# Second mixer's outputs: 32-partition chunk matrices turned by VectorE, 32x32 state tiles, two corrected chunks a step

## The reference, cut to what matters

```python
def step(s, inp):
    q_, w_, k_, v_, a_, b_ = inp
    sa = jnp.einsum('bhij,bhj->bhi', s, a_)
    s = s * w_[:, :, None, :] + sa[..., None] * b_[:, :, None, :] + v_[..., None] * k_[:, :, None, :]
    return (s, jnp.einsum('bhij,bhj->bhi', s, q_))
_, y = jax.lax.scan(step, s0, (qt, wt, kt, vt, at, bt))
...
y = ((yg - mu) / jnp.sqrt(var + EPS)).reshape(Bx, Tx, C) * ln_w + ln_b
y = y + (rk * v.reshape(Bx, Tx, H, HS)).reshape(Bx, Tx, C)
return y * g @ Wo.T
```

## Time and profile before

| what | value |
|---|---|
| median of 3 runs | 5464.05 us |
| the three runs | 5441.55, 5478.0, 5464.05 us |
| the profiled execution, first to last instruction | 5452.6 us |
| mean granted TensorE clock of it (1.0 is 2.4 GHz) | 0.926 |
| the changed stage in it | 4295.36 to 4500.67 us, 205.3 us |

### The profile page before, as it was taken

One profiled execution on the slowest core, in us unless ns is written; L12 is line 12 of the kernel. 1 busy time (PEld: TensorE's weight loads), 2 busy tenths in 40 slices (PEclk: granted clock), 3 DMA queues, 4 the chain that ended last, 5 costly groups with the idle time before them and its releaser, 6 DMA issues. The chain is left out here.

```text
span 5452.6 us, 104905 instructions
## 1 busy us (share of the span) xinstructions
PE 4831.1 (89%) x36890; PEld 3535.1 (65%) x36890; DVE 3836.5 (70%) x9111; ACT 2736.9 (50%) x6711; POOL 2285.8 (42%) x1860
## 2 busy tenths in 40 slices
PE   5999999999999999999889989984488778998998
PEld 3787777877777787777766556641156665654665
DVE  4766667777677766767578668746699657866874
ACT  2444445444544544545478658724400116875882
POOL 2434334344334434434267347514322116743751
PEclk7999999999999999999999999986699758998998
DMA  2000000000000000000100000000000000000000
GB/s 86 5 9 7 7 9 7 7 9 7 7 9 10 5 9 8 6 9 9 34 1 0 25 5 0 0 7 0 8 1 1 1 1 30 0 24 5 0 0 16
DMA packets 170085, 52.60 MB, mean 10 GB/s; under 512 B 142304, under 2 KB 166112, under 8 KB 168928
## 3 DMA queue, kind: packets, MB, share of 16 engines
q1 hardware_dynamic: 168160, 44.30, 3.7%
q10 hardware_dynamic: 1536, 3.21, 0.2%
HBM read 36.99 MB, written 10.49 MB: 9 GB/s over the span
## 5 line engine op out<-in xcount | busy, mean ns | idle before, releaser
L799 DVE SCALAR_TENSOR_TENSOR gd_qkT<-gd_ps,gd_w_qk,gd_qkT 128x256 f32<-128x256 f32 x768 | 367.2, 482 | 193.3 <-ACT gd_qkT L632 172.7
L984 POOL TENSOR_TENSOR gd_gV<-gd_g,cst 128x512 f32<-128x512 f32 x128 | 130.3, 1040 | 860.1 <-PE gd_ps L510 860.1
L417 PE MATMUL gd_ps<-gd_taps,gd_xwins 128*128 128x512 f32 x1024 | 465.3, 597 | 0.0
L676 ACT ACTIVATE gd_X<-gd_ps 128x512 f32<-128x512 f32 x384 | 201.1, 620 | 452.9 <-PE gd_ps L496 452.6
L1540 ACT ACTIVATE L_ffn_s<-L_ffn_s,L_ffn_nb,L_ffn_r 128x128 f32<-128x128 f32 x1024 | 419.4, 482 | 3.1
L1360 POOL TENSOR_TENSOR L_ffn_t<-L_ffn_t 128x512 f32<-128x512 f32 x128 | 190.2, 1486 | 391.8 <-DVE L_ffn_t L1581 391.8
L417 PEld LDWEIGHTS gd_ps<-gd_taps,gd_xwins 128*128 128x128 f32 x1024 | 192.8, 191 | 191.1 <-issue 185.6
L868 DVE TENSOR_TENSOR gd_Z<-gd_ps,cst 128x256 f32<-128x256 f32 x384 | 162.7, 424 | 129.6 <-PE gd_ps L512 111.1
L1579 DVE TENSOR_TENSOR L_ffn_t<-L_ffn_ps,L_ffn_sb_rope 128x512 f32<-128x512 f32 x256 | 176.8, 691 | 101.8 <-PE L_ffn_ps L1385 101.8
L521 PE MATMUL gd_ps<-gd_Z,gd_X 128*128 128x64 f32 x2048 | 239.2, 275 | 0.0
L512 PE MATMUL gd_ps<-gd_gV,gd_nA 128*128 128x64 f32 x2048 | 237.9, 275 | 0.0
(11 more groups left out here) (389 smaller groups left out, 13625.6 us busy)
## 6 DMA issues: line engine op xcount, KB each, us to landing
L_ffn_sb_rope<-in_rope SPq DMA_DIRECT2D x4, 2048.0 KB, 8.3
gd_tap_row<-in_L_attn_conv_v SPq DMA_DIRECT2D x2, 2048.0 KB, 15.6
gd_blocks<-gd_nA SPq DMA_DIRECT2D x256, 16.0 KB, 1.7
gd_Z<-gd_blocks SPq DMA_DIRECT2D x32, 128.0 KB, 2.0
gd_inverses<-gd_Z SPq DMA_DIRECT2D x32, 128.0 KB, 1.7
gd_gV<-gd_inverses SPq DMA_DIRECT2D x256, 16.0 KB, 1.9
L_ffn_sb_wqkv<-in_L_ffn_wqkv SPq DMA_DIRECT2D x4, 768.0 KB, 8.9
out<-out_tok SPq DMA_DIRECT2D x8, 256.0 KB, 2.6
```

Of the source, the lines that this page charges most:

```text
L417: ins = pe.matmul(ps[4 + i % 2][:], xwin(j)[:, t:t + P], taps[:, t, 512 * i:512 * (i + 1)], start=(t == 0), stop=(t == TAPS - 1))
L676: act.activation(heads(X, gi).rearrange("p h x -> p (h x)"), ps[4 + gi][:], ACT.Copy).then_inc(x_s.sem, 1)
L799: ins = dve.scalar_tensor_tensor(produced(j, i), ps[6 + i % 2][:, P + t:P + t + WIDE], w_tap[:, at, t:t + 1], produced(j, i), ALU.mult, AL ...
```

## The change

It does the following, all in `wkv_outputs`:

- The chunk matrices are spread within 32 partitions only (four heads of 8): `Ms`, 512 elements per partition for each k and b instead of 2048, with a mask `head4` that one added reduction makes from `head`. VectorE turns them itself, in blocks of 32x32, into `MT`, which now holds all 64 chunks. TensorE's turns, their PSUM tiles and ScalarE's copies are gone. All eight spreads and turns stand at the head of VectorE's list.
- A state's step multiplies four 32x32 tiles on the array's diagonal for each b (8 matmuls of 8 columns, 16 records) in place of one 128x128 (2 matmuls, 4 records). The two records for the chunk's own part stay.
- `corrected` does two chunks a call in place of four, for half blocks u of 8 states; there is one call in nearly every step from step 9 on (b = 0 and b = 1 by turns of four steps).
- GpSimd spreads states in halves (1024 elements, 16 of them in place of 8 of 2048).
- `normed` is split into `centred`, `sums` and `scaled`, with other work of VectorE between; the steps at which squares, roots, turns back and projections stand are given by constants. ScalarE takes one root at the start.

```diff
+SUB = 32
+AT_Y, AT_SQUARE, AT_ROOT, AT_TURN, AT_OUT = (9, 13), (22, 28), (25, 32), (28, 35), (32, 41)
...
+        MT = sb("MT", [P, B, CB, SUB])
+        Ms = [sb(f"Ms{b}", [P, BLK, SUB]) for b in range(B)]
...
+        quad = lambda r: slice(SUB * r, SUB * (r + 1))
+        half = BLK // 2
+        PACE = (CB - 1) + 3 * BLK
...
+                def turned_M(k, b):
+                    n = nth(k, b)
+                    src = S[:, b, RS:2 * RS, chunks(k)].rearrange("p j c -> p c j").unsqueeze(2).to_broadcast([P, BLK, SUB // RS, RS])
+                    mask = head4[:].unsqueeze(1).unsqueeze(3).to_broadcast([P, BLK, SUB // RS, RS])
+                    if k:
+                        dve.wait_ge(t_s, nth(k - 1, b) + 1)
+                    dve.tensor_tensor(Ms[b][:].rearrange("p c (h j) -> p c h j", j=RS), src, mask, ALU.mult).then_inc(m_s, 1)
+                    dve.wait_ge(m_s, n + 1)
+                    dve.transpose(MT[:, b, chunks(k)].rearrange("p c i -> p (c i)"), Ms[b][:].rearrange("p c j -> p (c j)")).then_inc(t_s, 1)
...
+                dve.tensor_reduce(head4[:], head.rearrange("p (g h) -> p h g", h=SUB // RS), AX_X, ALU.add).then_inc(h4_s, 1)
+                dve.wait_ge(h4_s, 1)
+                for k in range(NBLK):
+                    for b in range(B):
+                        turned_M(k, b)
+                for k in range(NBLK):
+                    centred(k, 0)
+                    if k:
+                        gated(k - 1, 1)
+                    sums(k, 0)
+                    scaled(k, 0)
+                    centred(k, 1)
+                    if k:
+                        residual(k - 1, 1)
+                    gated(k, 0)
+                    sums(k, 1)
+                    scaled(k, 1)
+                    residual(k, 0)
+                gated(NBLK - 1, 1)
+                residual(NBLK - 1, 1)
...
+                def advance(c):
...
                     pe.matmul(out, ident, S[:, :, 0:RS, c], start=True, stop=False)
-                    pe.wait_ge(ev_s, 8 * k + 2 * (j // 4) + 2)
+                    if c % BLK == 0:
+                        pe.wait_ge(t_s, nth(c // BLK, 1) + 1)
...
                     for b in range(B):
-                        ins = pe.matmul(out[:, b], MT[k % 2][:, b, j], S0[:, c, b], start=False, stop=(b == B - 1))
+                        for r in range(P // SUB):
+                            ins = pe.matmul(out[quad(r), b], MT[quad(r), b, c], S0[quad(r), c, b], start=False, stop=(b == B - 1))
...
+                def corrected(u, b, piece):
+                    k, n = u // 2, nth(u // 2, b)
+                    if piece == 0:
+                        pe.wait_ge(x_s, B * u + b + 1)
...
+                    for i in range(2):
+                        j = half * (u % 2) + 2 * piece + i
+                        q, at = j // 4, j % 4
+                        out = ps_y[b][CS * at:CS * (at + 1), P * q:P * (q + 1)]
...
+                for s in range(PACE):
+                    if s < CB - 1:
+                        advance(s)
+                    for b in range(B):
+                        u, piece = divmod(s - AT_Y[b], half)
+                        if 0 <= u < 2 * NBLK and piece < 4:
+                            corrected(u, b, piece)
+                    for b in range(B):
+                        k, at = divmod(s - AT_TURN[b], BLK)
+                        if at == 0 and 0 <= k < NBLK:
+                            turn_back(k, b)
+                        k, at = divmod(s - AT_OUT[b], BLK)
+                        if at == 0 and 0 <= k < NBLK:
+                            project(k, b)
...
+                act.activation(warm[:], eps[:], ACT.Sqrt, bias=eps[:], scale=1.0 / RS)
...
+                for u in range(2 * NBLK):
+                    at = slice(half * (u % 2), half * (u % 2 + 1))
+                    pool.wait_ge(st_s, half * u + half - 1)
                     for b in range(B):
...
+                        src = S0[:, half * u:half * (u + 1), b].unsqueeze(2).to_broadcast([P, half, RH, RS])
+                        mask = head.unsqueeze(1).unsqueeze(3).to_broadcast([P, half, RH, RS])
+                        pool.tensor_tensor(S0x[b][:, at], src, mask, ALU.mult).then_inc(x_s, 1)
```

More of the change, by code:

```diff
@@ L2350, in _, with centred @@
             def _(dve):
[L2351 to L2361, removed]
[L2362 to L2363 removed]
+                def turned_M(k, b):
+                    n = nth(k, b)
+                    src = S[:, b, RS:2 * RS, chunks(k)].rearrange("p j c -> p c j").unsqueeze(2).to_broadcast([P, BLK, SUB // RS, RS])
[5 more added lines that the diff above has]
+                    dve.transpose(MT[:, b, chunks(k)].rearrange("p c i -> p (c i)"), Ms[b][:].rearrange("p c j -> p (c j)")).then_inc(t_s, 1)
+                def centred(k, b):
+                    n = nth(k, b)
+                    dve.wait_ge(yc_mm[b], QUARTERS * (k + 1))
                     dve.tensor_reduce(mu[b][:], by_head(ps_y[b][:]), AX_X, ALU.add).then_inc(mu_s, 1)
@@ L2392, in _ @@
                 dve.memset(S0[:, 0], 0.0).then_inc(zero, 1)
[L2393 to L2403, removed]
+                dve.tensor_reduce(head4[:], head.rearrange("p (g h) -> p h g", h=SUB // RS), AX_X, ALU.add).then_inc(h4_s, 1)
[18 more added lines that the diff above has]
+                residual(NBLK - 1, 1)
             @block.tensor
             def _(pe):
[L2407 to L2413, removed]
-                        ins = pe.transpose(ps_t[g % 2][:, i], M[:, b, 4 * q + i].rearrange("p h j -> p (h j)"), ident)
-                    ins.then_inc(t_mm, 1)
-                def advance(k, j):
-                    c = BLK * k + j
+                def advance(c):
                     out = ps_s[c % 2][:, 0:B * RS].rearrange("p (b i) -> p b i", b=B)
@@ L2507, in _ @@
                 act.wait_ge(zero, 2)
-                for g in range(8):
-                    turned(0, g)
-                for k in range(NBLK + 2):
-                    for j in range(BLK):
-                        if BLK * k + j < CB - 1:
-                            state(BLK * k + j)
-                        if k + 1 < NBLK and j % 2 == 1:
-                            turned(k + 1, j // 2)
-                        if j in (9, 13):
-                            squares(k - 1, j // 13)
-                        if j in (10, 14):
-                            root(k - 1, j // 14)
+                act.activation(warm[:], eps[:], ACT.Sqrt, bias=eps[:], scale=1.0 / RS)
+                for s in range(PACE):
+                    if s < CB - 1:
+                        state(s)
+                    for b in range(B):
+                        k, at = divmod(s - AT_SQUARE[b], BLK)
+                        if at == 0 and 0 <= k < NBLK:
+                            squares(k, b)
+                        k, at = divmod(s - AT_ROOT[b], BLK)
+                        if at == 0 and 0 <= k < NBLK:
+                            root(k, b)
             @block.gpsimd
```

79 lines of the change are left out of this document (15 added, 64 removed).

## The result

The changed kernel took **5373.7 us** in the median of four runs (5361.3 to 5380.9), against 5459.0 for the kernel before on the same chip (5441.6 to 5478.0): a ratio of **0.9838**, 95% interval 0.9803 to 0.9874, or 85 us less.

What follows compares the result with a forecast made beforehand. It took TensorE's own order at the lower clock to bound the chain, plus waits for VectorE's spread matrices. Opening -9.2, chain steps -15.2 and end -4.7 summed to -29 us, so 5464 - 29 = 5435 us, range 5400 to 5470.

Steps and rivals of the forecast that it cites:

- I price everything at the lower level: Whole stage: TensorE's clock taken to stay at its lower level, 1.2 GHz, since gapless work had run at 0.50.
- The clock comes back: Rival, 6 in 100: 2.4 GHz granted in the stage, steps fall to about half, -58 on top, -87 in all, 5377.
- (b): State's product in a chain step: 16 records in four rounds of 0.1, 0.7 us to the copy, 0.63 to the next size.
- the own part: Chain step, the chunk's own two 128x128 records followed by another tile size: 0.58 us, bounds 0.38 to 0.61.
- bare steps: Chain's nine steps before the first call of `corrected`: 0.30 + 0.7 = 1.0 us each, 9.0 in all.
- The opening: Stage start to the first product with a state: 3.75 us against 12.95, so -9.2 us (-10 to -6.6).
- costs what a call of four costs, not half: Call of two chunks in a chain step: four rounds of 0.23, so 1.09 us; 32 more calls are 35 us.
- the waits cost nothing: Chain: waits for GpSimd's half spreads and VectorE's finishing work costed at nothing; uncovered, up to 2 us, four or five times.
- the six other pairs of spread and turn: VectorE's list: some 10 us, covered while TensorE does the first nine steps, so no cost; uncovered, 10 us once.
- The end: Last state to the last residual: 27 us against 31.7, so -4.7 us (23 to 31).
- The diagonal tiles run one behind another: Rival, 7 in 100: the product's sixteen records run serially; 5472 at pitch 0.06, 5632 at 0.23.
- Calls of two chunks cost half: Rival, 6 in 100: a call's time goes with its records, 0.6 us, 54 steps 27 us shorter, -56, so 5408.

Runs made afterwards that it cites:

- the wide product: Changed kernel with the state's product as two 128x128 matmuls on the identity in place of the narrow 32x32 ones: 5426.3 us, 0.9936.
- without the dense matmuls: Changed kernel with turns back and projections cut to 8 columns each, the rest of their tiles zeroed by VectorE: 5386.0 us, 0.9858.
- four chunks a call: Changed kernel with four chunks in each call of `corrected` and half as many calls: 5377.1 us, 0.9848.
- both wide versions: Changed kernel with the product as two 128x128 matmuls, alone (5426.3 us) and with two dense 128x512 matmuls in step 10 (5436.6 us, 0.9964).

## Why the prediction was wrong

**The step that failed** is in the reading of what bounds the kernel: "So being busy did not bring the clock back here, and I price everything at the lower level." The first half is true of the stretch that was read (4398 to 4430); it was no evidence for the second, since the change replaced the very matmuls of that stretch. And the clock had come back in that chain just before, as the projection at 4392.51 ended, and was gone again where the stretch that was read begins (busy time by engine, as in the earlier trace rows):

```profile
4394.40:4397.80 3.40, 1.98 (x18) 1.82 (x17) 3.40 (x2) 0.37 (x2) 0.00 (x0) 1.00 0.00 0
```

TensorE was busy for 1.98 of these 3.40 us, so a wait may have had its part in losing it. What the runs showed in place of that step: the clock does come back in the chain behind dense matmuls, and what follows decides whether it stays. With the wide product it is lost within three steps each time (three times in two runs, TensorE being busy throughout); with the narrow one and a call in each step it is held to the chain's end, for 52 steps in the longest case. The rival "The clock comes back", at 6 in 100, is what happened: 28 us in this execution, and its time, 5377, was near. That its sum came near is luck: it took 58 for the clock and 29 for the rest, and it was 28 and 59. The 58 supposed that steps fall to half; a step with a call fell from 1.89 to 1.17, by 38%, and 33 of the 63 steps did. "For it: no more waits of several us" wasn't the mechanism: without the dense matmuls there were no waits either, and the clock stayed.

**The second error is a size**, (b). The mechanism was right: sixteen records on four diagonal tiles go side by side. "I take rounds of 0.1, hence 0.7" and 0.63 to the next tile size were the term; measured 0.46 and 0.33, both below the bounds of 0.56 and 0.49. The rounds were too long, and the bound had kept 0.38 from the last record to the copy from 128x128 tiles. The records of this line that run at a time, in the product of the bare step above, and the line's records from 4310.5 to 4318 us (shortest, middle and longest, ns):

```profile
4310.87:4310.90 0.03, 0.03 (x4) 0.50 0.00 0
4310.95:4310.97 0.02, 0.02 (x8) 0.50 0.00 0
...
4311.05:4311.06 0.01, 0.01 (x16) 0.50 0.00 0
...
L2434 PE MATMUL wo_ps_s<-wo_S,wo_MT x144: 196/197/218, 4310.8 to 4318.0; 32*32 32x8 f32 x144
```

All four rounds have begun 0.20 after the first load at 4310.85, so a round is some 0.06 and not 0.1; a record is 0.2 long, and the copy starts 0.28 after the last round's start. In 53 steps that is 53 x 0.30 = 16 of the 26 us by which the steps at 0.50 were shorter; the call's 1.02 for 1.09 gives 3.7, the own part's 0.54 for 0.58 gives 2.1, bare steps of 0.87 for 1.0 give 1.2, a step too many (54 counted, where the chain ends at the last state's copy and holds 53) gives 2.3, and the turns back and projections, 10.6 for 12.2, the rest.

**What held.** The opening, 3.69 for 3.75, VectorE's turn at 0.71 for an estimate of 0.69. That a call of two "costs what a call of four costs, not half": 1.02 against 1.10. That the waits cost nothing: TensorE is busy throughout the chain. That the six other pairs of spread and turn are covered. The end, 23.5, lay at the low bound of 23 to 31; its first 11 us ran at 1.00, but with some 7 us at 1.00 it was 23.3 (four chunks a call) to 25.0 (both wide versions), so little of the gain is the clock's.

**The rivals.** "The diagonal tiles run one behind another" fell: sixteen records of 0.197 us each ran within 0.40. The Trainium skill's "TensorEngine Tiling (Array Packing)", section Restrictions and Gotchas, has it that different row tiles can't access one PSUM bank at the same time. The trace doesn't bear out the cost that the prediction drew from it: all four row tiles write `wo_ps_s`, one tile of 512 floats per partition, and sixteen of their records are under way at once. Whether two of them write in the same instant no row shows. The 50 ns a matmul that were estimated from the same page's Performance Considerations are more than these records take: all sixteen loads are through in 0.30 us, 19 ns each on average. "Calls of two chunks cost half" fell with 1.02.

**The chances.** 12 in 100 for faster by over 1% was too little, because the clock's 6 rested on one stretch of the old kernel, and no bound of (b) went below 0.49.

**What stays open**: why the narrow product holds the clock and the wide one doesn't, though TensorE is busy without a gap under both; and which of the dense matmuls brings it back. With the narrow product that was the first turn back in two executions, the projection of step 32, 41, 48 or 57 in others, and none in the chain with four chunks a call alone; with the wide one two projections of one execution and none of the other.

## What to carry to other kernels

A clock read in a stretch belongs to the instructions of that stretch: where a change replaces them, price the sum at both levels and give the second a real chance. Before counting a saving in instructions, look at which of them run side by side: half a call's records were worth 0.08 of 1.10 us, while sixteen records on four diagonal tiles took 0.33 us where four wide ones took 0.93. Where one step uses two tile sizes, try it with one: the own part as four diagonal tiles gave 0.26 to 0.43 us a step with a call, more than the 0.17 that such a step was forecast to gain by the change under study. Compare the changed stage, not the span, when the effect is smaller than what the unchanged rest varies by (42 us here).

## What the runs showed of the hardware that was not expected

- Removing dense matmuls made the stage longer (137.5 us for 118.1), and adding two that nobody reads made it shorter (107.2); the medians go the same way (5386, 5374 and 5356 us), with intervals that overlap.
- One added 128x512 matmul (2.1 us at the lower clock) did not bring the clock back, two in a row (3.6 us) did, in the three profiled executions that had them; a single projection of the same size, later in the chain, did in some executions and not in others.
- Steps of the same kernel differ by 1.6 times (1.89 and 1.17 us) within one execution, and the point of change differed by 12 steps from one execution to the next; a mean by line hides this.
- One 128x128 matmul of 16 columns (two records) in front of the 32x32 tiles cost more than the eight 32x32 records that take its place: 0.43 us a step at the lower clock and 0.26 at the full one. Whether the load or the change of size costs it isn't shown.
